# Adding the second results to a stored output with accumulating memory-to-memory transfers

## Chip, cores and metric

The kernel runs on one core of one Trainium2 chip. The metric is the device time of one execution in microseconds (us). Five engines take part: TensorE (PE), VectorE (DVE), ScalarE (ACT), GpSimd (POOL) and SyncE (SP). They run their own instruction streams and wait for one another through semaphores. SP, ACT and POOL also issue DMA transfers.

## What is computed

The input `x` has 16 images of 16 by 16 positions with 128 channels, so 4096 normalised tokens for the expert part: 2 experts of 8 are chosen for each token.

```python
x = x + conv(_ln_c(x))              # attention-like mixing inside each image
t = x.reshape(16, 256, 128)         # x here is called x1 in the kernel
logits = tn @ Wg                    # tn = _ln_t(t)
top_logits, top_idx = top_k(logits, 2);  top_w = softmax(top_logits)
for the two chosen experts e:
    y_e = (silu(tn @ W1[e]) * (tn @ W3[e] + b3[e])) @ W2[e]
out = t + top_w[0] * y_first + top_w[1] * y_second
```

## The kernel before

The first part works through 8 units of 512 tokens (4 tiles of 128): normalisation, mixing, x1, the choice of experts, and a scatter of each token's row, twice, into `sorted_rows` in main memory, ordered by expert. x1 stays in SBUF, in `x1_all`.

The second part runs over 71 slots (`NS`), each a tile of 128 rows of one expert. SP loads the rows of a slot into one of 8 buffers `xs`. TensorE, ScalarE and VectorE compute the expert's result. ScalarE writes the weighted result in two parts (`y_parts`), GpSimd adds the two parts into one of 8 buffers `ys` (L1192) and scatters the 128 rows to `result_rows` in main memory with an indirect DMA (L1195). The semaphore `y_out[b]` counts the scatters of buffer b. `result_rows` holds for each token two rows: the result of its first expert at the token's number, that of its second expert `TOK` = 4096 rows further on.

The experts are worked through in order, and the kernel's structure lets the first half of `result_rows` be complete a few slots before the second: the table `first_half` says how many scatters of each ring buffer must have landed for it.

The last part adds the results to x1 and stores the output. It is the part that the change touches. Its steps are:

- SP waits for the scatters that the first half needs (`half_table`, L472 and on), then issues eight loads of 256 KB (`load_results(u, 0)`, L461), one for each unit, into the tile `both`. That tile lies in the room of the expert weights, `w_all`, which are no longer needed; the profile therefore names it `w_all`. A load on one of four semaphores waits for the load four units earlier.
- VectorE adds each unit's first half to x1 in place (`add_half`, L1143) and counts `half_ready`.
- SP waits for all scatters (L479) and issues eight more loads, of the second half.
- VectorE adds x1 to each of these in place and counts `res_ready`.
- ACT stores each unit (`store`, L852) when its `res_ready` has come, and waits for all stores (`out_done`).

Loads and stores of this part have contiguous pieces of 1 KB: two tokens of 128 floats for each of 128 partitions and two images.

GpSimd has nothing to do after its last scatter. An engine runs its stream in order: GpSimd's scatters of the last slots stand in front of anything that comes behind them.

Of the kernel before, what the change touches and what calls it, by code (L numbers as in the profile page):

```python
# [34 lines left out]
ALU = mybir.AluOpType  # L35
# [3 lines left out]
P = 128  # L39
# [4 lines left out]
def ds(start, size):  # L44
    return slice(start, start + size) if isinstance(start, int) else bass.ds(start, size)
# [33 lines left out]
def build(nc, x, Wq, bq, Wk, bk, Wv, bv, Wr, br, Wg, W1, W2, W3, b3, out):  # L79
    B, H, W, C = x.shape  # L80
    TOK = B * H * W
    NT = TOK // P
    DIM = Wq.shape[1]
    VDIM = Wk.shape[1]
    E, _, F = W1.shape
    TPU = 4
    NU = NT // TPU
    IMG = H * W
    K = 2
    KF = F // P  # L90
    REGION = TOK + P
    NS = (K * TOK + E * (P - 1)) // P
# [3 lines left out]
    RING = 8  # L96
    LAST_RING = 4
# [2 lines left out]
    assert E == NU  # L100

    x_tok = x.rearrange("b h w c -> (b h w) c").rearrange("(b p s) c -> p b (s c)", p=P, s=2)
    out_tok = out.rearrange("b h w c -> (b h w) c").rearrange("(b p s) c -> p b (s c)", p=P, s=2)

    sorted_rows = nc.dram_tensor("sorted_rows", [E * REGION + SPARE * P, ROW], F32)
    result_rows = nc.dram_tensor("result_rows", [K * TOK + (E + SPARE) * P, P], F32)

    with ExitStack() as ctx:
        def sb(name, shape, dt=F32):
            return ctx.enter_context(nc.sbuf_tensor(name, shape, dt))  # L110

        def sem(name):
            return ctx.enter_context(nc.semaphore(name))
# [38 lines left out]
        x1_all = x_all  # L152
# [68 lines left out]

        w_flat = w_all[:].rearrange("p e j f -> p (e j f)")
        UC = TPU * C
        both = w_flat[:, 0:NU * K * UC]
        ys = [w_flat[:, NU * K * UC + i * P:NU * K * UC + (i + 1) * P] for i in range(RING)]
        assert NU * K * UC + RING * P <= E * 3 * F
        y_parts = [sb(f"y_parts{i}", [P, 2, C]) for i in range(2)]


# [84 lines left out]
        y_sum = sem("y_sum")  # L314
        y_out = [sem(f"y_out{i}") for i in range(RING)]

        y_in = [[sem(f"y_in{i}_{k}") for k in range(K)] for i in range(LAST_RING)]
        half_ready = sem("half_ready")
        res_ready = sem("res_ready")
        out_done = sem("out_done")  # L320

        POOL_CONSTS = 8
# [4 lines left out]
        def at_least(eng, semaphore, value):  # L327

            if not (isinstance(value, int) and value <= 0):
                eng.wait_ge(semaphore, value)  # L330
# [59 lines left out]
        @block.sync  # L390
        def _(sp):
            def load_x(u):

                at_least(sp, x_in[u.par], u.half * 16)
                sp.dma_start(x_all[:, ds(u.n * TPU, TPU), :].rearrange("p (b s) c -> p b (s c)", s=2),
                             x_tok[:, ds(u.n * 2, 2), :]).then_inc(x_in[u.par], 16)

            load_x(Step(0, 0))
            for dst, src in ((wkv[:, 0:VDIM], Wk), (wkv[:, VDIM:P], Wv),
                             (bkv[0:VDIM, :], bk.unsqueeze(1)), (bkv[VDIM:P, :], bv.unsqueeze(1))):  # L400
                sp.dma_start(dst, src).then_inc(kv_in, 16)
            for u in range(1, 4):
                load_x(Step(0, u))
            sp.dma_start(w_all[:, :, 0, :], W1.rearrange("e c f -> c e f")).then_inc(expert_in, 16)
            sp.dma_start(w_all[:, :, 1, :], W3.rearrange("e c f -> c e f")).then_inc(expert_in, 16)
            for k in range(KF):
                sp.dma_start(w_all[:, :, 2, k * C:(k + 1) * C],  # L407
                             W2[:, k * P:(k + 1) * P, :].rearrange("e p d -> p e d")).then_inc(expert_in, 16)
            with sp.Fori(2, NU // 2) as q:
                load_x(Step(q, 0))  # L410
                load_x(Step(q, 1))
            sp.dma_start(b3_all[:].rearrange("p e f -> p (e f)"),
                         b3.rearrange("e f -> (e f)").partition_broadcast(P)).then_inc(b3_in, 16)

            sp.wait_ge(pool_consts, POOL_CONSTS)
            for i in range(SPARE):
                first = E * REGION + i * P
                sp.dma_start(sorted_rows[first:first + P, :], pad_rows[:, E + i, :]).then_inc(pads_in, 16)


            def free_rows(u):
                sp.wait_ge(scattered[u.par], u.half * (16 * SCATTERS) + 16 * SCATTERS)
                sp.sem_inc(rows_free, 1)

            sp.sem_inc(rows_free, 2)
            with sp.Fori(0, NU // 2 - 1) as q:
                free_rows(Step(q, 0))
                free_rows(Step(q, 1))

            sp.wait_ge(count_ready, 1)  # L430
            for e in range(E):
                n_rows = sp.value_load(count_i[0:1, e:e + 1], min_val=0, max_val=TOK)
                sp.dma_start(sorted_rows[ds(n_rows + e * REGION, P), :], pad_rows[:, e, :]).then_inc(pads_in, 16)
            sp.wait_ge(table_ready, 1)

            def load_rows(q, b):
                s = q * RING + b

                at_least(sp, y_out[b], q * 16)
                first = sp.value_load(slot_row[0:1, ds(s, 1)], min_val=0, max_val=E * REGION + (SPARE - 1) * P)  # L440
                if isinstance(s, int) and s == 0:

                    sp.wait_ge(pads_in, 16 * (E + SPARE))
                    for i in range(2):
                        sp.wait_ge(scattered[i], 16 * SCATTERS * (NU // 2))
                sp.dma_start(xs[b][:], sorted_rows[ds(first, P), :]).then_inc(xs_in[b], 16)

            for b in range(RING):
                load_rows(0, b)
            with sp.Fori(1, NS // RING) as q:  # L450
                for b in range(RING):
                    load_rows(q, b)
            for b in range(NS % RING):
                load_rows(NS // RING, b)


            def load_results(u, k):

                at_least(sp, y_in[u.ring][k], u.round * 16)
                src = result_rows[ds(u.n * TPU * P + k * TOK, TPU * P), :]  # L460
                sp.dma_start(both[:, ds((u.n * K + k) * UC, UC)].rearrange("p (b m) -> p b m", b=2),  # L461
                             src.rearrange("(b p s) c -> p b (s c)", p=P, s=2)).then_inc(y_in[u.ring][k], 16)

            def load_half(k):
                for o in range(LAST_RING):
                    load_results(Slot(0, o, LAST_RING, NU), k)
                with sp.Fori(1, NU // LAST_RING) as q:
                    for o in range(LAST_RING):
                        load_results(Slot(q, o, LAST_RING, NU), k)


            sp.wait_ge(half_table, 1)  # L472
            for b in range(RING):
                count = sp.value_load(first_half[0:1, b:b + 1], min_val=16, max_val=16 * ((NS + RING - 1) // RING))
                wait_in_front(sp, waited_sp, (y_out[b], count))
            load_half(0)

            for b in range(RING):
                sp.wait_ge(y_out[b], 16 * ((NS - b + RING - 1) // RING))  # L479
            load_half(1)  # L480


        @block.tensor
# [203 lines left out]
        def _(act):  # L687
# [159 lines left out]
            run_slots(act, step, copy_rows_t)  # L847


            def store(u):  # L850
                act.wait_ge(res_ready, u.n + 1)
                act.dma_start(out_tok[:, ds(u.n * 2, 2), :],  # L852
                              both[:, ds((u.n * K + 1) * UC, UC)].rearrange("p (b m) -> p b m", b=2)
                              ).then_inc(out_done, 16)

            with act.Fori(0, NU // 2) as q:
                store(Step(q, 0))
                store(Step(q, 1))
            act.wait_ge(out_done, 16 * NU)


        @block.vector
        def _(dve):
# [270 lines left out]

            run_slots(dve, step, split_rows)

            def add_half(u, k, done):
                x1 = x1_all[:, ds(u.n * TPU, TPU), :].rearrange("p t c -> p (t c)")
                y = both[:, ds((u.n * K + k) * UC, UC)]
                dve.wait_ge(y_in[u.ring][k], u.round * 16 + 16)  # L1140
                if k == 1:
                    dve.wait_ge(half_ready, NU)
                nc.vector.tensor_tensor(y if k == 1 else x1, x1, y, ALU.add).then_inc(done, 1)  # L1143

            for k, done in ((0, half_ready), (1, res_ready)):
                with dve.Fori(0, NU // LAST_RING) as q:
                    for o in range(LAST_RING):
                        add_half(Slot(q, o, LAST_RING, NU), k, done)


        @block.gpsimd
        def _(pool):
# [52 lines left out]
            for n in range(NS // RING * RING, NS):  # L1205
                scatter_results(Slot(0, n, RING, NS))


INPUTS = ("x", "L0_conv_Wq", "L0_conv_bq", "L0_conv_Wk", "L0_conv_bk", "L0_conv_Wv", "L0_conv_bv", "L0_conv_Wr",
          "L0_conv_br", "L0_ffn_Wg", "L0_ffn_W1", "L0_ffn_W2", "L0_ffn_W3", "L0_ffn_b3")  # L1210
# [17 lines left out]
```

## Time and profile before

| | us |
|---|---|
| median of 3 runs | 347.84 |
| lowest, highest | 346.51, 349.89 |
| the profiled execution, its own time | 349.18 |
| its span, first to last instruction | 347.4 |
| last scatter of results issued at | 328.73 |
| last store of the output issued at | 344.8 |

The span is what the trace shows; the execution's own time has a little around it. TensorE is busy for 268.4 us of the span (77%), VectorE 243.7 (70%), ScalarE 183.7 (53%) and GpSimd 176.4 (51%). Times in rows are counted from the span's start. The busy time of a DMA-issuing instruction on SP or ACT says only how long the issue took; when the data landed is told by "DMA to landing".

### The profile page before, as it was taken

The page shows a single profiled execution, that of the slowest core. Times are in us where ns is not written, and L with a number is a line of the kernel's source. Part 1 is how long each engine was busy: PE and PEld are TensorE (multiplying, and loading weights), DVE is VectorE, ACT ScalarE, POOL GpSimd, SP SyncE. Part 2 cuts the span into 40 slices and gives each one's busy share as a digit, 9 for nine tenths or more (in the row PEclk, how much of TensorE's full clock was granted, in tenths as well). Part 3 has the DMA queues.
Part 4 walks back from the last instruction along what each step waited for, and adds up shares of the span by engine and source line. Part 5 has one row for each costly group of instructions (what it writes and reads, how often), then busy time and mean ns, then how long its engine had stood idle before and what let it go on. Part 6 is the DMA issues. An engine that isn't in the chain of part 4 may idle for free.

```text
span 347.4 us, 7832 instructions
## 1 busy us (share of the span) xinstructions
PE 268.4 (77%) x1723; PEld 218.3 (63%) x1724; DVE 243.7 (70%) x811; ACT 183.7 (53%) x464; POOL 176.4 (51%) x221
## 2 busy tenths in 40 slices
PE   1988888868877851869898999999898979989200
PEld 0444555635544531359798999989898969888100
DVE  3357988788897457228687787888787858867633
ACT  3446654645753431026576676767676757766100
POOL 4000055744767757603666666666666556666600
PEclk9999989889999886769999999999999999999755
DMA  3997201101111112320212212211212212123668
GB/s 114 322 311 246 53 27 37 54 31 38 39 40 47 54 33 69 93 55 15 60 49 64 61 52 55 61 54 52 61 53 53 61 46 61 47 61 91 214 214 277
DMA packets 31811, 29.75 MB, mean 86 GB/s; under 512 B 4992, under 2 KB 29504, under 8 KB 31664
## 3 DMA queue, kind: packets, MB, share of 16 engines
q1 hardware_dynamic: 24704, 18.38, 18.7%
q0 software_dynamic: 4320, 8.92, 7.8%
q10 hardware_dynamic: 2768, 2.23, 1.9%
q8 instruction: 7, 0.11, 0.2%
q14 instruction: 12, 0.10, 0.1%
HBM read 17.51 MB, written 12.01 MB: 85 GB/s over the span
## 4 chain that ended last, share of the span: by engine, by line
POOL 22%; PE 21%; issue 19%; DMA 14%; DVE 12%; SPq 6%; ACT 3%; POOLq 1%; DVEq 1%; ACTq 0%
POOL result_rows L1195 11%; POOL w_all L1192 7%; POOL sorted_rows L1175 4%; DMA result_rows<-w_all,xs 4%; DMA xs<-sorted_rows 3%; DMA w_all<-result_rows 3%; PE bank L579 3%; SPq L407 3%; DMA x_all<-x_dram 3%; PE bank L645 2%; PE bank L663 2%; ACT row_buf L742 2%; PE bank L646 2%; PE bank L647 2%; PE bank L539 2%
## 5 line engine op out<-in xcount | busy, mean ns | idle before, releaser
L1175 POOL DMA_INDIRECT sorted_rows<-row_buf,position x64 | 65.1, 1018 | 76.1 <-DVE seen L1020 41.5
L1195 POOL DMA_INDIRECT result_rows<-w_all,xs x71 | 72.2, 1017 | 59.3 <-POOL w_all L1192 57.1
L579 PE MATMUL bank<-all_ones 128*128 128x512 bf16 x205 | 63.7, 422 | 13.3 <-DMA bkv<-L_conv_bv_dram 7.7
L645 PE MATMUL bank<-w_up,xs_hi 128*128 x142 | 55.1, 388 | 7.4 <-issue 7.4
L1098 DVE TENSOR_TENSOR gate<-bank,b_all 128x384 f32<-128x384 f32 x71 | 39.6, 558 | 29.9 <-PE bank L647 29.1
L663 PE MATMUL bank<-w_down,act_hi 128*128 x213 | 58.7, 344 | 0.8 <-ACT y_parts L833 0.8
L647 PE MATMUL bank<-w_up,xs_hi 128*128 x142 | 48.9, 344 | 0.0
L646 PE MATMUL bank<-w_up,xs_lo 128*128 x142 | 48.9, 344 | 0.0
L828 ACT ACTIVATE act_hi<-bank 128x384 fp32r<-128x384 f32 x71 | 34.8, 491 | 26.5 <-PE bank L653 26.1
L665 PE MATMUL bank<-w_down,act_lo 128*128 x213 | 47.6, 223 | 0.0
L1106 DVE TENSOR_TENSOR act_rows<-silu_h,gate 128x384 f32<-128x384 f32 x71 | 44.2, 622 | 3.1
L1192 POOL TENSOR_TENSOR w_all<-y_parts 128x128 f32<-128x128 f32 x71 | 35.4, 498 | 17.3 <-ACT y_parts L833 15.2
L823 ACT ACTIVATE silu_h<-bank 128x384 f32<-128x384 f32 x71 | 34.9, 492 | 15.5 <-PE bank L647 14.9
L579 PEld LDWEIGHTS bank<-all_ones 128*128 128x128 bf16 x205 | 19.7, 109 | 34.0 <-issue 19.1
L663 PEld LDWEIGHTS bank<-w_down,act_hi 128*128 128x128 f32 x213 | 40.1, 188 | 1.3 <-issue 1.1
L665 PEld LDWEIGHTS bank<-w_down,act_lo 128*128 128x128 f32 x213 | 40.8, 192 | 0.0
L833 ACT ACTIVATE y_parts<-bank,xs 128x256 f32<-128x256 f32 x71 | 33.6, 474 | 12.4 <-PE bank L665 10.2
L1118 DVE TENSOR_TENSOR act_lo<-bank,act_hi 128x384 fp32r<-128x384 f32 x71 | 38.9, 548 | 0.7 <-ACT act_hi L828 0.7
L653 PE MATMUL bank<-ident,act_rows 128*128 128x128 f32 x213 | 35.2, 274 | 0.3 <-DVE act_rows L1106 0.3
L645 PEld LDWEIGHTS bank<-w_up,xs_hi 128*128 128x128 f32 x142 | 28.4, 200 | 9.2 <-issue 9.1
L1112 DVE TENSOR_TENSOR xs_lo<-bank,xs_hi 128x128 fp32r<-128x128 f32 x71 | 20.3, 285 | 15.1 <-ACT xs_hi L818 13.2
L742 ACT ACTIVATE row_buf<-x_all,shift,rstd 128x256 f32<-128x256 f32 (+1 forms) x32 | 17.3, 591 | 23.4 <-DVE shift L921 19.5
(137 smaller groups left out, 427.6 us busy)
## 6 DMA issues: line engine op xcount, KB each, us to landing
xs<-sorted_rows SPq DMA_DIRECT2D x71, 65.0 KB
w_all<-result_rows SPq DMA_DIRECT2D x16, 256.0 KB, 4.4
w_all<-L_ffn_W_dram SPq DMA_DIRECT2D x2, 1536.0 KB, 8.8
x_all<-x_dram SPq DMA_DIRECT2D x8, 256.0 KB, 4.0
out_dram<-w_all ACTq DMA_DIRECT2D x8, 256.0 KB, 4.3
w_all<-L_ffn_W_dram SPq DMA_DIRECT2D x3, 512.0 KB, 11.3
b_all<-L_ffn_b_dram SPq DMA_DIRECT2D x1, 1536.0 KB, 8.1
result_rows<-w_all,xs POOLq DMA_INDIRECT x71, 2.3
```

Source lines behind the costliest of these rows:

```text
L579: nc.tensor.matmul(bank[free_bank][:].rearrange("p (a b) -> p a b", a=4), all_ones[:], all_ones[:].unsqueeze(1).broadcast_to([P, 4, P]), s ...
L645: nc.tensor.matmul(o, xs_hi[s.par][:], w[0], start=True, stop=False)
L646: nc.tensor.matmul(o, xs_lo[s.par][:], w[0], start=False, stop=False)
L647: nc.tensor.matmul(o, xs_hi[s.par][:], w[1], start=False, stop=True).then_inc((h_ps, g_ps)[j], 1)
L663: nc.tensor.matmul(bank[7][:, 0:2 * C], act_hi[s.par][:, k * P:(k + 1) * P], w, start=(k == 0), stop=False)
L665: last = nc.tensor.matmul(bank[7][:, 0:C], act_lo[s.par][:, k * P:(k + 1) * P], w[:, 0:C], start=False, stop=(k == KF - 1))
L1098: nc.vector.tensor_tensor(gate[s.par][:], bank[3 + s.par][:, 0:F], b3_all[:, ds(e, 1), :].rearrange("p a f -> p (a f)"), ALU.add).then_inc ...
L1106: nc.vector.tensor_tensor(act_rows[s.par][:], silu_h[s.par][:], gate[s.par][:], ALU.mult).then_inc(act_ready, 1)
L1118: nc.vector.tensor_tensor(act_lo[s.par][:], bank[5 + s.par][:, 0:F], act_hi[s.par][:].bitcast(F32), ALU.subtract).then_inc(act_lo_ready, 1)
L1175: nc.gpsimd.indirect_dma_start(out=sorted_rows.ap(), out_offset=bass.IndirectOffsetOnAxis(ap=position[u.par][:, c:c + 1], axis=0), in_=row ...
L1192: nc.gpsimd.tensor_tensor(ys[s.ring][:], y_parts[s.par][:, 0, :], y_parts[s.par][:, 1, :], ALU.add).then_inc(y_sum, 1)
L1195: nc.gpsimd.indirect_dma_start(out=result_rows.ap(), out_offset=bass.IndirectOffsetOnAxis(ap=xs[s.ring][:].bitcast(I32)[:, DEST:DEST + 1], ...
```

## The change

The second halves are no longer loaded. When VectorE has added the first half of a unit to x1, ACT stores that sum to the output. When all scatters have landed, GpSimd issues for each unit one transfer from `result_rows` straight to the output, in main memory, with `accum_op=ALU.add`: the transfer adds its source to what stands in the output. For unit u it waits for `half_out[u]`, the landing of that unit's store. Each of these transfers covers 256 KB in 128 pieces of 2 KB, contiguous on both sides. GpSimd, and no longer ACT, waits for the end. The loops of ACT and GpSimd over the units are written out.

```diff
-        both = w_flat[:, 0:NU * K * UC]
-        ys = [w_flat[:, NU * K * UC + i * P:NU * K * UC + (i + 1) * P] for i in range(RING)]
+        first_halves = w_flat[:, 0:NU * UC]
+        ys = [w_flat[:, NU * UC + i * P:NU * UC + (i + 1) * P] for i in range(RING)]
...
-            load_half(0)
-
-            for b in range(RING):
-                sp.wait_ge(y_out[b], 16 * ((NS - b + RING - 1) // RING))
-            load_half(1)
+            load_first_half()
...
-            def store(u):
-                act.wait_ge(res_ready, u.n + 1)
-                act.dma_start(out_tok[:, ds(u.n * 2, 2), :],
-                              both[:, ds((u.n * K + 1) * UC, UC)].rearrange("p (b m) -> p b m", b=2)
-                              ).then_inc(out_done, 16)
-
-            with act.Fori(0, NU // 2) as q:
-                store(Step(q, 0))
-                store(Step(q, 1))
-            act.wait_ge(out_done, 16 * NU)
+            for u in range(NU):
+                act.wait_ge(half_ready, u + 1)
+                act.dma_start(out_tok[:, u * 2:u * 2 + 2, :],
+                              x1_all[:, u * TPU:(u + 1) * TPU, :].rearrange("p (b s) c -> p b (s c)", s=2)
+                              ).then_inc(half_out[u], 16)
...
-            for k, done in ((0, half_ready), (1, res_ready)):
-                with dve.Fori(0, NU // LAST_RING) as q:
-                    for o in range(LAST_RING):
-                        add_half(Slot(q, o, LAST_RING, NU), k, done)
+            with dve.Fori(0, NU // LAST_RING) as q:
+                for o in range(LAST_RING):
+                    add_first_half(Slot(q, o, LAST_RING, NU))
...
+            for b in range(RING):
+                pool.wait_ge(y_out[b], 16 * ((NS - b + RING - 1) // RING))
+            for u in range(NU):
+                pool.wait_ge(half_out[u], 16)
+                rows = slice(u * TPU * P, (u + 1) * TPU * P)
+                pool.dma_start(out_rows[rows, :].rearrange("(p s) c -> p (s c)", p=P),
+                               result_rows[TOK + u * TPU * P:TOK + (u + 1) * TPU * P, :]
+                               .rearrange("(p s) c -> p (s c)", p=P), accum_op=ALU.add,
+                               max_dma_last_dim=2048).then_inc(out_done, 16)
+            pool.wait_ge(out_done, 16 * NU)
```

## Rows read from the trace of the kernel before

**Rows 1.** The page: busy tenths in 40 slices of the span

```profile
PE   1988888868877851869898999999898979989200
...
ACT  3446654645753431026576676767676757766100
POOL 4000055744767757603666666666666556666600
...
DMA  3997201101111112320212212211212212123668
```

**Rows 2.** Chain of waits, 327 to 348: start us, us, what

```profile
328.73 2.53 DMA result_rows<-w_all,xs
...
331.40 0.38 SPq L461
...
332.85 4.76 DMA w_all<-result_rows
...
337.63 5.94 DMA w_all<-result_rows
...
343.84 0.69 DVE w_all L1143
```

**Rows 3.** Windows of the end: stretch, length, busy by engine, PEclk, DMA share, GB/s

```profile
324.00:326.00 2.00, 0.03 (x1) 0.00 (x0) 1.59 (x3) 0.47 (x1) 1.38 (x2) 0.76 0.82 252
326.00:328.00 2.00, 0.00 (x0) 0.00 (x0) 1.43 (x3) 0.00 (x0) 1.66 (x2) 0.50 0.69 245
328.00:330.00 2.00, 0.00 (x0) 0.00 (x0) 1.12 (x2) 0.00 (x0) 1.25 (x1) 0.50 0.09 31
...
329.00:330.00 1.00, 0.00 (x0) 0.00 (x0) 0.12 (x1) 0.00 (x0) 0.98 (x1) 0.50 0.00 0
...
330.00:331.30 1.30, 0.00 (x0) 0.00 (x0) 0.00 (x0) 0.00 (x0) 0.00 (x0) 0.50 0.15 50
...
337.60:343.60 6.00, 0.00 (x0) 0.00 (x0) 3.04 (x5) 0.00 (x0) 0.00 (x0) 0.50 1.03 351
```

**Rows 4.** DMA queues in 332.6 to 347.4: packets, MB, share of 16 engines

```profile
DMA packets 4338, 4.18 MB, mean 282 GB/s; under 512 B 256, under 2 KB 4338, under 8 KB 4338
...
q1 hardware_dynamic: 2162, 2.08, 44.4%
q10 hardware_dynamic: 2176, 2.10, 40.2%
```

**Rows 5.** Timeline from 318, and the stores (L852): durations ns, starts, landing

```profile
322.50 1.39 DVE L1143 TENSOR_TENSOR x_all<-x_all,w_all  x2
...
324.07 0.47 ACT L833 ACTIVATE y_parts<-bank,xs 128x256 f32<-128x256 f32 x1 [1.19 <-PE bank L665]
324.40 2.98 DVE L1143 TENSOR_TENSOR x_all<-x_all,w_all  x4 [0.52 <-DMA w_all<-result_rows]
327.83 1.29 DVE L1143 TENSOR_TENSOR x_all<-x_all,w_all  x2 [0.45 <-DMA w_all<-result_rows]
...
L852 ACTq DMA_DIRECT2D out_dram<-w_all x8: 389/391/426, 335.5 to 344.8; - x8
...
DMA to landing us min/median/max: 2.2/4.3/4.9
```

**Rows 6.** Loads (L461); scatters (L1195) from 315 on; the scatter in 318.5 to 319

```profile
L461 SPq DMA_DIRECT2D w_all<-result_rows x16: 372/392/552, 318.4 to 337.6; - x16
...
L1195 POOL DMA_INDIRECT result_rows<-w_all,xs x7: 982/1163/1253, 314.2 to 328.7; - x7
...
DMA to landing us min/median/max: 2.2/3.4/4.5
...
DMA to landing us min/median/max: 4.5/4.5/4.5
```

More of the change, by code:

```diff
@@ L102, in build @@
     x_tok = x.rearrange("b h w c -> (b h w) c").rearrange("(b p s) c -> p b (s c)", p=P, s=2)
+    out_rows = out.rearrange("b h w c -> (b h w) c")
     out_tok = out.rearrange("b h w c -> (b h w) c").rearrange("(b p s) c -> p b (s c)", p=P, s=2)
@@ L223, in build @@
         UC = TPU * C
-        both = w_flat[:, 0:NU * K * UC]
-        ys = [w_flat[:, NU * K * UC + i * P:NU * K * UC + (i + 1) * P] for i in range(RING)]
-        assert NU * K * UC + RING * P <= E * 3 * F
+        first_halves = w_flat[:, 0:NU * UC]
+        ys = [w_flat[:, NU * UC + i * P:NU * UC + (i + 1) * P] for i in range(RING)]
+        assert NU * UC + RING * P <= E * 3 * F
         y_parts = [sb(f"y_parts{i}", [P, 2, C]) for i in range(2)]
@@ L315, in build @@
         y_out = [sem(f"y_out{i}") for i in range(RING)]
-        y_in = [[sem(f"y_in{i}_{k}") for k in range(K)] for i in range(LAST_RING)]
+        y_in = [sem(f"y_in{i}") for i in range(LAST_RING)]
         half_ready = sem("half_ready")
-        res_ready = sem("res_ready")
+        half_out = [sem(f"half_out{i}") for i in range(NU)]
         out_done = sem("out_done")
@@ L454, in _, with load_results, load_first_half @@
                 load_rows(NS // RING, b)
[L457 to L464, printed above, removed]
+            def load_results(u):
+                at_least(sp, y_in[u.ring], u.round * 16)
+                src = result_rows[ds(u.n * TPU * P, TPU * P), :]
+                sp.dma_start(first_halves[:, ds(u.n * UC, UC)].rearrange("p (b m) -> p b m", b=2),
+                             src.rearrange("(b p s) c -> p b (s c)", p=P, s=2)).then_inc(y_in[u.ring], 16)
+            def load_first_half():
                 for o in range(LAST_RING):
-                    load_results(Slot(0, o, LAST_RING, NU), k)
+                    load_results(Slot(0, o, LAST_RING, NU))
                 with sp.Fori(1, NU // LAST_RING) as q:
                     for o in range(LAST_RING):
-                        load_results(Slot(q, o, LAST_RING, NU), k)
+                        load_results(Slot(q, o, LAST_RING, NU))
             sp.wait_ge(half_table, 1)
@@ L1135, in _, with add_first_half @@
             run_slots(dve, step, split_rows)
-            def add_half(u, k, done):
+            def add_first_half(u):
                 x1 = x1_all[:, ds(u.n * TPU, TPU), :].rearrange("p t c -> p (t c)")
[L1139 to L1143, printed above, removed]
-            for k, done in ((0, half_ready), (1, res_ready)):
-                with dve.Fori(0, NU // LAST_RING) as q:
-                    for o in range(LAST_RING):
-                        add_half(Slot(q, o, LAST_RING, NU), k, done)
+                dve.wait_ge(y_in[u.ring], u.round * 16 + 16)
+                nc.vector.tensor_tensor(x1, x1, first_halves[:, ds(u.n * UC, UC)], ALU.add).then_inc(half_ready, 1)
+            with dve.Fori(0, NU // LAST_RING) as q:
+                for o in range(LAST_RING):
+                    add_first_half(Slot(q, o, LAST_RING, NU))
         @block.gpsimd
```

## The prediction

> **What bounds the kernel now.** I read the page first for the shape of the run. In forty slices [rows 1] the DMA engines are lightly used for most of the span and fill up only at its start and in the last four slices, in the last two of which TensorE, ScalarE and GpSimd do nothing. So the end is a stage of its own, and the change touches only it. The chain of waits over the last 20 us [rows 2] says what orders it. GpSimd adds the two parts of a tile (L1192) and scatters its rows (L1195); the last scatter is issued at 328.73 and its data are confirmed 2.53 us later, at 331.26. Only then may SP start reading the second half of the results. It issues eight loads, the chain waits on them (4.76 and 5.94 us), VectorE makes one last addition (0.69 us), and the last store runs out to 347.4. From the landing of the last scatter to the end that is 16.1 us, 4.6% of the span. This is all that the change can shorten.
>
> The windows [rows 3] show what fills these 16.1 us: from 332.6 to the end the DMA engines move 4.18 MB, eight loads of 256 KB and eight stores of as much. By queue [rows 4], SP's loads take 44.4% of 16 engines over these 14.8 us, 6.6 us of full use, and ACT's stores 40.2%, 5.9 us. The transfers alone are 12.5 us; the other 3.6 us are SP's issue and the first latency (331.3 to 332.6), some idle time and the last landing. VectorE's eight additions (L1143) lie beside transfers, but for the last one. In 337.6 to 343.6 the engines are full at 351 GB/s [rows 3]. So the end is bound by bytes, with a latency at each side, and a change in it is to be priced in passes of 2.1 MB over the DMA engines, each about 6 us.
>
> **The change, part by part.** Times are on the clock of the profiled execution (span 347.4); its own time is 349.18, so 1.8 us lie around the span, and the median of the runs is 347.84. I add the difference that I get to the median.
>
> *What goes.* The eight second loads (6.6 us of the engines), the second additions (8 by 0.69 us, of which only the last is on the path) and the eight stores after them (5.9 us). SP's wait for all scatters (L479) goes too. SP has nothing behind it. The smaller buffer `first_halves` moves the scatter buffers `ys` to other columns, which costs nothing.
>
> *What moves: the stores, now of x1 plus the first halves.* They run from ACT after each first addition. ACT's last piece of work ends at 324.07+0.47 = 324.5 [rows 5], two additions are done by then, so the first store goes at about 324.7. The additions go on until 329.12 [rows 5], and the last store goes just behind. VectorE and ACT issue costs (0.39 us a store [rows 5]) lie under the additions. The bytes don't lie under nothing, though: the engines are at a share of 0.82 in 324 to 326 and 0.69 in 326 to 328 with the first loads and scatters, and only 0.09 and 0.15 afterwards [rows 3]. If the store data begin at 326, there is 1.4 us of load and scatter work in 326 to 328, 0.4 us in 328 to 331.3, and 5.9 us of stores: the engines are full until about 326+7.7 = 333.7. No store bounds the end by itself; GpSimd needs `half_out[0]` first, and that was stored long ago.
>
> What it costs is the last scatter, which now lands among stores. Issued at 328.73 it took 2.53 us with idle engines [rows 2]. Of the scatters among the first loads one took 4.5 us, and the median of the last seven is 3.4 [rows 6]. So its landing is 0.9 to 2.0 us later: I take 1.5, at 332.8. If the stores keep out of its way it is 0. Everything queued behind it on GpSimd, all eight accumulating transfers, waits for it. Here the trace agrees with the Trainium skill (DMA: Bandwidth & Descriptors, "Issuing engines are not separate DMA queues"), which says that transfers from all queues run on the same 16 engines and interleave.
>
> *What is added: eight accumulating transfers from GpSimd, memory to memory.* Each moves 256 KB, 128 pieces of 2 KB. The kernel before has none of this kind, so there are two prices to bound.
>
> The first is GpSimd's time for one. From below, SP's and ACT's issue of a 256 KB transfer, 0.39 us [rows 5, 6]; from above, GpSimd's own row that makes 128 addresses, 0.98 us at the least and 1.25 us beside VectorE [rows 2, 6]. VectorE is silent then. I take 1.0 plus 0.15 for the waits and register work between. Eight are 9.2 us.
>
> The second is the time on the DMA engines. An addition must read the source, read the output rows, and write them: two reads and one write for 2.1 MB each. From below it costs one pass, 5.9 to 6.6 us (the second read hidden). From above it costs three, since a load or a store of the kernel before touches main memory once and this touches it three times: 18.8 us. Between these I take two passes, because each engine must read twice what it writes: 12.5 us. That is more than GpSimd's 9.2, so GpSimd runs ahead and its issue is hidden but for the first.
>
> By the Trainium skill (Collectives: The Full Stack, "The bandwidth ceiling: the fold count and why AG ≠ RS ≠ AR") an addition in a transfer halves the rate since it needs two source reads, and the addition itself is free; that is the two passes. No row here shows it.
>
> *The sum.* The last scatter lands at 332.8. The first accumulating transfer's data begin 1.6 us after its issue, as the last scatter's do (issued 328.73, no bytes until 330 [rows 2, 3]): 334.4, when the stores are just gone. Two passes, 12.5 us: 346.9. Idle time in between: before, it was 14.8−12.5 = 2.3 us with VectorE in the loop; here the queue is kept full, I take a quarter, 0.6: 347.5. From the last data to the end of the span, 0.7 us (the last store was issued at 344.8 and took at least 2.2 us to land [rows 5], and the span ends at 347.4): 348.2. Before it is 347.4, so +0.8, and on the median 348.6 us. One latency hop and one pass of stores leave the end; half a microsecond to two come back by the late scatter, and the second read of the output rows eats the pass saved. No change that could be told.
>
> **Rivals.** *The addition costs one pass (chance 0.24).* If the second read hides under the write, the data take 6.3 us and GpSimd's issue is the bound: 332.8 + 7 × 1.15 = 340.9 for the last issue, then 2.2 us as the last store took, 0.9 more for GpSimd's slower issue, and 0.4 to the end: 344.4, that is −3.0 and 344.8 us. With an issue of 0.45 us the data bind: 334.4+6.3+0.7 = 341.4, 341.8 us; with 1.25 us and gaps of 0.15 it is 346.5 us. For it: loads and stores together ran at 351 GB/s, so reading and writing do go on at once. Against: nothing shows one engine reading two streams at that rate. Somewhat over half of this case lies beyond 1%.
>
> *Memory traffic binds (chance 0.34), the case on the other side.* Place: the eight accumulating transfers. If every touch of main memory costs what it did before, three passes are 18.8 us: 334.4+18.8+0.7 = 353.9, +6.5, 354.3 us. It makes the kernel slower by over 1% once the data take 16 us or more, under 131 GB/s of results. For it: in the kernel before no transfer goes from memory to memory, so the 351 GB/s were never asked of memory alone; the 128 pieces of a transfer also each wait for a read before the write can go. Against: if the two sides of memory are not shared with the engines' own limit, the third touch is free. The Trainium skill (DMA: Bandwidth & Descriptors, "Latency and other measured facts") has plain copies between memory tensors at 207 to 214 GB/s in each direction at best. At that rate one plain copy of 2.1 MB would be 10 us and three touches instead of two 15 us, which would end about 3 us later than before. No run here shows it.
>
> *Something else (0.06)*: the addition works off one piece after another at well over three passes.
>
> **How the numbers follow.** My forecast (two passes) has 0.36: 348.6 us, on its own 345.5 to 351.5, the low end with the scatter on time, no idle time and data 8% faster, the high one with the scatter 0.5 us later still, 1.2 us more idle time and data 10% slower. One percent of the median, about what a measurement of this kernel can tell from no change, is 3.5 us: 344.4 and 351.3. Faster by over 1%: 0.15 from one pass and 0.05 from the forecast, 0.20. Slower by over 1%: 0.29 from three passes, 0.06 from the last case and 0.03 from the forecast, 0.38. Within: 0.42. The range runs from 343.5 (a one-pass addition with a cheap issue, beyond which I leave some 0.08) to 356 (three passes with the late scatter at its worst, beyond which 0.10).
>
> **What the profile after would show.** ACT's stores from about 324.7 to 329.6, and DMA share near 1 until 333 or so. The last scatter landing 3.4 to 4.5 us after its issue instead of 2.53. Eight GpSimd transfers about 1.15 us apart from 332.9. Then the stretch from the first accumulating data to the last: near 6 to 9 us is one pass, 12 to 13 two, 18 or more three. If GpSimd's issues lie more than 1.6 us apart, it is GpSimd that binds, which I give little room. My forecast is wrong above all if that stretch is not 12.5 us; a scatter that is not late moves it by 1.5 us.

## The result and the profile after

The changed kernel is slower. Its median is 352.93 us (351.24 to 355.08, 4 runs) against 347.55 us (346.51 to 349.89, 4 runs) of the kernel before, a ratio of 1.0193 with a 95% interval of 1.0138 to 1.0248. The ratio is estimated from the fast runs and is not the quotient of the two medians, which is 1.0155. The time lies inside the whole forecast range (343.5 to 356), but above the forecast of 348.6 us, above that forecast's own 345.5 to 351.5, and above the 351.3 us up to which the prediction spoke of no change.

The page of the kernel after shows busy tenths in 40 slices of a span of 349.2 us, as [rows 1] does for the kernel before:

```profile
POOL 4000055745767677216666666666666566666530
DMA  4998101111111113211122122122212121229790
```

The last digit of the DMA row is a 0. For the last slice, 8.7 us, almost nothing is transferred, and no engine computes, yet the span goes on. The chain of waits (start us, us, what) in 322 to 350, to be compared with [rows 2], ends at 334.9 and says nothing of the last 14 us:

```profile
322.77 4.40 DMA result_rows<-w_all,xs
...
327.98 6.89 POOL out_dram L1201 x8
```

The windows of the same trace, columns as in [rows 3]:

```profile
322.80:327.20 4.40, 0.00 (x0) 0.00 (x0) 1.38 (x2) 0.00 (x0) 0.96 (x1) 0.50 1.07 379
327.20:330.00 2.80, 0.00 (x0) 0.00 (x0) 0.00 (x0) 0.00 (x0) 2.02 (x4) 0.50 0.26 35
330.00:341.60 11.60, 0.00 (x0) 0.00 (x0) 0.00 (x0) 0.00 (x0) 4.87 (x6) 0.50 1.00 178
341.60:349.20 7.60, 0.00 (x0) 0.00 (x0) 0.00 (x0) 0.00 (x0) 0.00 (x0) 0.50 0.00 0
```

The accumulating transfers fill the engines from 330 to 341.6 at 178 GB/s of results, and then 7.6 us follow with nothing at all. What these are is told by the sequencers' own instructions on the line of the closing block. Columns: line, engine, instruction, count, duration in ns least/median/most, first and last start. First after, then before, and with the latter GpSimd's last scatter (start us, us):

```profile
L109 POOLq COMPARE_BRANCH  x1: 38/38/38, 341.6 to 341.6; - x1
L109 POOLq DRAIN  x1: 7176/7176/7176, 341.8 to 341.8; - x1
```

```profile
L108 POOLq DRAIN  x1: 8012/8012/8012, 328.5 to 328.5; - x1
...
L108 ACTq COMPARE_BRANCH  x1: 38/38/38, 347.0 to 347.0; - x1
L108 ACTq DRAIN  x1: 8/8/8, 347.2 to 347.2; - x1
...
328.73 1.25 POOL L1195 DMA_INDIRECT result_rows<-w_all,xs  x1 [0.81 <-POOL w_all L1192]
```

Each engine ends its program with an instruction called DRAIN, the closing drain. On ACT it took 8 ns in the kernel before, on GpSimd 7 to 8 us. In the kernel before GpSimd's sequencer took up the drain at 328.5, while the last scatter still stood in front of it; the scatter's row ends at 330.0, and the drain was through at 336.5, 6.5 us later and eleven microseconds before the end. In the changed kernel GpSimd is the engine that waits for the last transfers (`out_done`), so its drain starts after them, at 341.8, and nothing lies beside it.

The stretch from the issue of the last scatter to the end of the span, step by step:

| us | before | after | difference |
|---|---|---|---|
| last scatter, issue to landing | 2.5 | 4.4 | +1.9 |
| landing to the next transfer's issue | 0.1 | 0.8 | +0.7 |
| that issue to the last landing | 15.6 | 13.6 | −2.0 |
| last landing to the end of the span | 0.4 | 7.6 | +7.2 |
| sum | 18.7 | 26.4 | +7.7 |

The accumulating transfers did save 2 us here. The late scatter took them back, and the drain costs 7.2. The stretch is 7.7 us longer, but the spans differ by only 1.8 (349.2 and 347.4). In this execution of the changed kernel the last scatter was issued 6.0 us sooner, at 322.77. Nothing before it was changed, and experiment e8 treats it.

### The profile page after: what moved, and what is told of

It is laid out like the page before. It is cut to its first block, busy times and chain, and to the rows that moved or that the text cites. A ratio compares the mean times of both kernels' runs of the same rounds, so it can differ in the third digit from the quotient of the medians.

```text
span 349.2 us, 7747 instructions
## 1 busy us (share of the span) xinstructions
PE 265.1 (76%) x1723; PEld 215.3 (62%) x1724; DVE 239.1 (68%) x803; ACT 183.7 (53%) x464; POOL 183.9 (53%) x229
## 3 DMA queue, kind: packets, MB, share of 16 engines
q0 software_dynamic: 5472, 11.02, 11.2%
## 4 chain that ended last, share of the span: by engine, by line
POOL 32%; issue 23%; PE 14%; DVE 12%; DMA 9%; ACT 4%; POOLq 1%; SPq 1%; DVEq 1%; ACTq 0%
POOL result_rows L1183 15%; POOL w_all L1180 9%; POOL sorted_rows L1163 5%; PE bank L576 4%; DMA result_rows<-w_all,xs 3%; DMA xs<-sorted_rows 2%; DMA sorted_rows<-row_buf,position 2%; POOL out_dram L1201 2%; ACT row_buf L739 2%; DMA bkv<-L_conv_bv_dram 1%; DVE stats L886 1%; PE bank L526 1%; DVE x_all L950 1%; PE bank L501 1%; DVE stats L875 1%
## 5 line engine op out<-in xcount | busy, mean ns | idle before, releaser
L576 PE MATMUL bank<-all_ones 128*128 128x512 bf16 x205 | 62.8, 417 | 13.0 <-DMA bkv<-L_conv_bv_dram 7.6
L642 PE MATMUL bank<-w_up,xs_hi 128*128 x142 | 54.4, 383 | 7.2 <-issue 7.2
L644 PE MATMUL bank<-w_up,xs_hi 128*128 x142 | 48.5, 341 | 0.0
L1098 DVE TENSOR_TENSOR act_rows<-silu_h,gate 128x384 f32<-128x384 f32 x71 | 45.0, 634 | 3.1
L820 ACT ACTIVATE silu_h<-bank 128x384 f32<-128x384 f32 x71 | 35.0, 493 | 13.8 <-PE bank L644 12.3
L1104 DVE TENSOR_TENSOR xs_lo<-bank,xs_hi 128x128 fp32r<-128x128 f32 x71 | 20.2, 284 | 15.3 <-ACT xs_hi L815 12.5
L739 ACT ACTIVATE row_buf<-x_all,shift,rstd 128x256 f32<-128x256 f32 (+1 forms) x32 | 17.3, 590 | 23.7 <-DVE shift L913 16.1
```

The lines of the kernel that those rows point to most:

```text
L576: nc.tensor.matmul(bank[free_bank][:].rearrange("p (a b) -> p a b", a=4), all_ones[:], all_ones[:].unsqueeze(1).broadcast_to([P, 4, P]), s ...
L642: nc.tensor.matmul(o, xs_hi[s.par][:], w[0], start=True, stop=False)
L644: nc.tensor.matmul(o, xs_hi[s.par][:], w[1], start=False, stop=True).then_inc((h_ps, g_ps)[j], 1)
L1098: nc.vector.tensor_tensor(act_rows[s.par][:], silu_h[s.par][:], gate[s.par][:], ALU.mult).then_inc(act_ready, 1)
```

## Experiments

Each kernel's times stand beside runs of the kernel before on the same chip. The level differs: beside e1 to e4 and e9b the kernel before took about 370 us, beside the others 347 to 348, and the granted clock of the profiled runs is 0.86 to 0.88 there against 0.90 to 0.92. The difference arises before the first result scatter, which is issued at 182.8 to 185.8 in the traces of the 370 us level and at 156.4 to 162.9 in the others; from there to the last one it takes 165 to 168 us at both. What sets the level isn't known. The stretch from the last scatter's issue to the end has hardly any TensorE work in it, and I compare that across the levels ("the end stretch" below: 18.7 us before, 26.4 after). It and the ratio answer one question in two ways. The kernel before was traced once, at the 348 us level; e2 and e9b show how far the same transfers can differ from it. All the numbers first (us, but for the ratio):

| kernel | median, before beside it | ratio (95%) | last scatter issued, span | end stretch |
|---|---|---|---|---|
| e1 | 376.48, 369.86 | 1.0165 (1.0112 to 1.0217) | 353.6, 375.9 | 22.3 |
| e2 | 377.60, 369.86 | 1.0224 (1.0177 to 1.0271) | 353.0, 377.2 | 24.2 |
| e3 | 373.88, 369.86 | 1.0129 (1.0064 to 1.0195) | 350.0, 371.4 | 21.4 |
| e4 | 377.04, 369.86 | 1.0202 (1.0154 to 1.0250) | 350.2, 376.1 | 25.9 |
| e5 | 355.08, 347.81 | 1.0165 (1.0096 to 1.0234) | 328.7, 353.2 | 24.5 |
| e6 | 347.42, 347.81 | 0.9974 (0.9933 to 1.0016) | 326.8, 345.9 | 19.1 |
| e7 | 353.84, 347.81 | one run, none | 325.3, 351.8 | 26.5 |
| e8 | 354.99, 347.81 | 1.0178 (1.0123 to 1.0234) | 326.9, 353.1 | 26.2 |
| e10 | 350.33, 347.45 | 1.0076 (1.0021 to 1.0131) | 328.3, 347.7 | 19.4 |
| e9b | 371.27, 370.78 | 1.0010 (0.9975 to 1.0044) | 353.2, 371.0 | 17.8 |

### e2: the closing drain exposed in the kernel before

```diff
-            act.wait_ge(out_done, 16 * NU)
...
+            pool.wait_ge(out_done, 16 * NU)
```

> The kernel before, with one edit: the wait for the stores of the output stands on GpSimd instead of ACT. No transfer and no computation is changed. Theory (closing drain): GpSimd's drain of 7 to 8 us now begins when the last store has landed, so the kernel is slower by about 7 us, 2.0%: near 355 us. Rival a (drain takes its time only for transfers in flight; none are left by then): under 1 us slower. Rival b: no change.

One wait was moved from one engine to another, and the kernel became 2.2% slower (at least 1.8%). The closing instructions in its trace:

```profile
L108 POOLq COMPARE_BRANCH  x1: 38/38/38, 370.3 to 370.3; - x1
L108 POOLq DRAIN  x1: 6527/6527/6527, 370.5 to 370.5; - x1
```

The last store has landed at 370.3, and the drain still takes 6.5 us though GpSimd has nothing in flight. The end stretch is 24.2 us, 5.5 more than in the kernel before; the medians differ by 7.7. The stretch has two parts. From the last store's landing to the end of the span it is 6.9 us against 0.4. From the last scatter's issue to that landing it is 17.3 us against 18.3, a microsecond less with the same transfers. Both rivals fall, and this edit alone has the size of the whole loss. For the saving of the change it says this: loads and stores take 14.7 us here from the first load's issue to the last landing, and 15.6 in the trace before, so the changed kernel's 13.6 us save 1 to 2 us.

### e1: ACT waits for the accumulating transfers

```diff
                               ).then_inc(half_out[u], 16)
+            act.wait_ge(out_done, 16 * NU)
...
-            pool.wait_ge(out_done, 16 * NU)
```

> The changed kernel, but ACT and not GpSimd waits for the accumulating transfers. Theory (closing drain): in the changed kernel GpSimd's closing drain of 7.2 us stands behind its wait for the transfers, with nothing beside it; here it begins when the last transfer is issued (334.9 in the changed kernel's trace, landing 341.6) and lies beside the data. If the drain runs its course from the last issue, as in the kernel before (it ended 6.5 us after the last scatter was issued), it ends near 342 and the kernel is 6 to 7 us faster than the changed one: about 345 us. Rival a (the drain starts its work only when GpSimd's own transfers have landed): the end stays within 1.5 us of the changed kernel. Rival b (the drain has no part in the slower time, the accumulating transfers alone are dear): no change to the changed kernel, 352 us.

The end stretch fell from 26.4 to 22.3 us: by 4, not by 6 to 7, and not by under 1.5 either. The ratio of 1.0165 overlaps that of the changed kernel, so it doesn't separate the two, and e4, with the changed kernel's end on the same chip, is only 0.6 us slower in its median. The trace shows why my expectation failed. The landing row is that of the accumulating transfers, in us:

```profile
L109 POOLq DRAIN  x1: 14472/14472/14472, 361.2 to 361.2; - x1
L109 ACTq COMPARE_BRANCH  x1: 38/38/38, 372.0 to 372.0; - x1
...
L1202 POOL DMA_DIRECT2D out_dram<-result_rows x8: 973/1940/3051, 358.3 to 362.2; - x8
...
DMA to landing us min/median/max: 4.1/6.9/9.9
```

ACT is through at 372.0. GpSimd's drain began at 361.2 and ends at 375.7, 3.6 us after GpSimd's own last transfer landed (362.2+9.9 = 372.1). So this drain did not end before GpSimd's transfers had landed, and had some 3.6 us left then. With GpSimd's as the last transfer of the kernel, 3.6 us stay exposed though ACT waits.

### e4: does the drain pay for each transfer?

```diff
             scatter_rows(Step(0, NU - 1))
+            pool.drain()
```

> The changed kernel with one more drain on GpSimd, after its scatters of sorted rows (64 of them), where it idles for 14 us. It tells what the closing drain's 7.2 us are for. Theory (the drain works through each transfer that GpSimd issued since the last drain, 143 in the changed kernel, about 50 ns each): the closing drain falls to 79/143 of 7.2 us, 4.0 us, the early one takes about 3 us where it is hidden, and the kernel is 3.2 us faster than the changed one. Rival (a fixed price for each drain): the closing drain stays at 7.2 us, the kernel at its time; slower, if the early drain delays the first result scatter.

```profile
L1175 POOLq DRAIN  x1: 13992/13992/13992, 154.5 to 154.5; - x1
```

```profile
L109 POOLq DRAIN  x1: 6516/6516/6516, 369.3 to 369.3; - x1
```

The closing drain took 6.5 us with 79 transfers since the last one, and the same 6.5 us with 135 in e2; with 143 it took 7.2. The theory wanted 4.0 and a price in proportion to the transfers, and that is refuted. The early one began at 154.5 while scatters were still queued in front of it (the last one started at 162.2 and took 0.96 us) and was through at 168.5, 5.3 us later, well before the first result scatter at 185.0. It cost nothing that can be seen (end stretch 25.9), and it brought nothing. A fixed price isn't shown either: from GpSimd going free to the end of the drain it took 5.3 us with 64 transfers since the last drain, 6.5 with 79 or 135, and 7.2 with 143.

### e3: plain copies, the addition of the second halves left out

```diff
-                               .rearrange("(p s) c -> p (s c)", p=P), accum_op=ALU.add,
+                               .rearrange("(p s) c -> p (s c)", p=P),
```

> The changed kernel with plain copies in place of the accumulating ones: the addition of the second halves is left out, the output is the second half alone. Theory (an addition costs two passes over the DMA engines, a copy one): the share of the engines that GpSimd's eight transfers take falls from 12.1 us to about 6 us, GpSimd's issue (0.98 us at least, eight of them) becomes the bound of this stretch, and the end is 3 to 4 us sooner. Rival (memory traffic or the pieces of 2 KB set the pace, not the second read): under 2 us sooner, the rate stays near 200 GB/s.

GpSimd's queue in e3, from the first issue to the last landing (354.1 to 364), and below it the same of the changed kernel (327.9 to 341.7). Columns: packets, MB, share of 16 engines:

```profile
q0 software_dynamic: 640, 2.10, 60.0%
```

```profile
q0 software_dynamic: 1152, 2.10, 87.4%
```

A copy takes 60.0% of 9.9 us, 5.9 us of full use; an addition 87.4% of 13.8 us, 12.1 us. That is a factor of 2.03. From memory to memory a copy costs no more than a load or a store of the same bytes did before (5.9 to 6.6 us, from [rows 4]), and the addition costs one more pass. One rival remains in these two rows: the copies also went in fewer packets (640 against 1152). e7 meets it. First issue to last landing fell from 13.6 to 9.7 us, 3.9 as the theory said. The issue row of the copies shows that GpSimd was not the bound even then:

```profile
L1201 POOL DMA_DIRECT2D out_dram<-result_rows x8: 526/526/592, 354.2 to 357.9; - x8
```

They start 0.53 us apart. The expectation had named GpSimd's issue as the bound at 0.98 us each; that part is wrong.

### e7: pieces of 8 KB

```diff
-                pool.dma_start(out_rows[rows, :].rearrange("(p s) c -> p (s c)", p=P),
+                pool.dma_start(out_rows[rows, :].rearrange("(p s) c -> p (s c)", p=32),
                                result_rows[TOK + u * TPU * P:TOK + (u + 1) * TPU * P, :]
-                               .rearrange("(p s) c -> p (s c)", p=P), accum_op=ALU.add,
-                               max_dma_last_dim=2048).then_inc(out_done, 16)
+                               .rearrange("(p s) c -> p (s c)", p=32), accum_op=ALU.add,
+                               max_dma_last_dim=8192).then_inc(out_done, 16)
```

> The changed kernel with the accumulating transfers in 32 pieces of 8 KB instead of 128 of 2 KB. Theory (the price is the two reads): the engines' use stays near 12 us, the landing of the last transfer 13 to 14 us after the first issue. Rival (the price is per piece): a fourth of the pieces cuts it below 9 us. A fourth of the pieces also cuts what GpSimd's part of each transfer takes. If the closing drain depends on the number of pieces in GpSimd's queue it falls below 6 us; if it is a fixed price it stays at 6.5 to 7.2.

With a fourth of the pieces the transfers take 78.8% of 14.2 us, 11.2 us of full use instead of 12.1, and the last one lands 14.1 us after the first issue (344.2 against 330.1). The closing drain is 7.2 us. The queue's packets fell from 1152 to 384, fewer than the 640 of e3's copies, and yet the engines were used for 1.9 times as long as by the copies. So neither pieces nor packets explain the second pass; they move the price by 7%, and the time not at all. GpSimd's part of a single transfer hardly changed either (0.93 us at the least against 0.98).

### e5: without the early stores (the output lacks x1 plus the first halves)

```diff
-            for u in range(NU):
-                act.wait_ge(half_ready, u + 1)
-                act.dma_start(out_tok[:, u * 2:u * 2 + 2, :],
-                              x1_all[:, u * TPU:(u + 1) * TPU, :].rearrange("p (b s) c -> p b (s c)", s=2)
-                              ).then_inc(half_out[u], 16)
+            act.wait_ge(half_ready, NU)
...
-                pool.wait_ge(half_out[u], 16)
```

> The changed kernel with ACT's stores of x1 plus the first halves left out (the output lacks that part) and GpSimd's waits for them gone. Theory (the last scatter lands late because stores fill the DMA engines): it lands 2.5 us after its issue, as in the kernel before, and not 4.4 as in the changed kernel; the eight accumulating transfers are unchanged at 12.1 us of the engines, and from the last scatter's issue to the end of the span it takes 24 to 24.5 us instead of 26.4. Rival (the lateness comes from the first loads, or from chance): the landing stays at 3.4 to 4.5 us.

The chain of waits of e5:

```profile
328.72 2.50 DMA result_rows<-w_all,xs
```

Without the stores the last scatter lands 2.50 us after its issue, as in the kernel before (2.53, [rows 2]); with all of them it took 4.4, 3.9 (e1), 3.4 (e3), 4.4 (e4), 4.0 (e7) and 3.9 (e8). The end stretch is 24.5 us. So the stores beside it delay the last scatter by 0.9 to 1.9 us. This is the price of storing early.

### e8: the changed kernel again

No edit.

> The changed kernel unchanged, beside the kernel before on the same chip. In the first trace of it the last scatter was issued 6.0 us sooner than in the trace before, though nothing before it was changed. Theory (these 6.0 us are chance, from the granted clock of the earlier stages, and the change costs what the stretch after the last scatter's issue shows): the ratio is that of 26.4 against 18.7 us, 7.7 us or 2.1 to 2.2%, and the stretch is 26.4 within 0.5 us. Rival (the earlier stages are really faster with the changed kernel, by 6 us): the ratio is 1.005.

The end stretch is 26.2 us and the ratio 1.0178, which is 6.2 us, with 4.3 to 8.1 as its interval; the 7.7 us of the end stretch lie inside. In this trace the last scatter is issued at 326.9, in the first trace of the same code at 322.8, in that of the kernel before at 328.7. The place of the last scatter moves by 4 us between two executions of one code, and the ratio does not have the 1.005 that a really faster start would give. Most of the 6.0 us lie far ahead of the change, as the scatters of results show (first and last start; first trace, then e8; the kernel before begins at 161.3):

```profile
L1183 POOL DMA_INDIRECT result_rows<-w_all,xs x71: 982/985/1367, 156.4 to 322.8; - x71
...
L1183 POOL DMA_INDIRECT result_rows<-w_all,xs x71: 982/982/1363, 161.4 to 326.9; - x71
```

4.9 us of the 6.0 were there before the first result was scattered. They come from no edit and did not return in e8: chance. The expectation put them down to the granted clock, but its mean is 0.918 in the first trace and 0.919 in that of the kernel before. What set them stays open.

### e6 and e10: two or four of eight units by GpSimd, ACT waits for the end

```diff
+        BY_POOL = 2
...
+            for u in range(BY_POOL, NU):
+                sp.dma_start(second_halves[:, u * UC:(u + 1) * UC].rearrange("p (b m) -> p b m", b=2),
...
+            act.wait_ge(res_out, 16 * (NU - BY_POOL))
+            act.wait_ge(out_done, 16 * BY_POOL)
...
-            for u in range(NU):
+            for u in range(BY_POOL):
                 pool.wait_ge(half_out[u], 16)
```

In e10 `BY_POOL` is 4. ACT's early stores run over the first `BY_POOL` units as well, and the other units' second halves go through SP, VectorE and ACT as in the kernel before.

> A mix meant to keep the changed kernel's gain without the exposed drain: units 0 and 1 go the changed kernel's way (stored early, accumulating transfer from GpSimd, 2 of 8), units 2 to 7 the way of the kernel before (second half loaded, added by VectorE, stored by ACT); ACT waits for the end. Theory (closing drain, and two passes either way): GpSimd is free 13 us before the end, its drain is hidden, the late scatter costs under 1 us more than in the kernel before, and the last scatter's issue to the end takes 17.5 to 18.5 us against 18.7 before: within 0.5% of the kernel before, and 2% faster than the changed one. Rival (GpSimd's transfers share the engines and land late, and 3.6 us of drain follow them): 20 us or more.

> The mix with four units instead of two by GpSimd's accumulating transfers. Theory (the closing drain cannot end sooner than 3.6 us after GpSimd's last transfer has landed): GpSimd's transfers share the engines with loads and stores and land within 2 us of the last store, so 2 to 3.5 us of the drain are exposed, and the last scatter's issue to the end takes 20.5 to 22 us against 19.1 with two units. Rival (the drain is hidden whenever ACT is the one that waits): 19 us.

The closing instructions, e6 and then e10:

```profile
L109 POOLq DRAIN  x1: 12673/12673/12673, 330.4 to 330.4; - x1
L109 ACTq COMPARE_BRANCH  x1: 38/38/38, 345.5 to 345.5; - x1
```

```profile
L109 POOLq DRAIN  x1: 14801/14801/14801, 332.7 to 332.7; - x1
L109 ACTq COMPARE_BRANCH  x1: 38/38/38, 346.4 to 346.4; - x1
```

In e6 GpSimd's last transfer lands at 339.7, the drain ends 3.4 us later, at 343.1, and ACT ends the kernel at 345.5: all hidden. Against the changed kernel on the same chip (e8) it is 2.0% faster (0.9974 against 1.0178), and against the kernel before it is no different. Its end stretch, 19.1 us, missed the 17.5 to 18.5 that I expected. In e10 the last transfer lands at 344.0, the drain ends at 347.5, again 3.5 us later, and ACT was done at 346.4. 1.1 us are exposed, where I expected 2 to 3.5, and the end stretch of 19.4 us is below my range. The ratio rose by 1.0% over e6, 3.5 us across two chips, but the end stretch by only 0.3; the rest of that rise isn't explained by the traces. So the drain's place came out as forecast in both traces, and the sizes did not. The last scatter was not late in either (2.41 and 2.39 us) with two or four early stores.

### e9b: a version that might beat both

```diff
-            load_half(1)
+            for u in range(NU):
+                sp.dma_start(both[:, (u * K + 1) * UC:(u * K + 2) * UC].rearrange("p (b m) -> p b m", b=2),
+                             result_rows[TOK + u * TPU * P:TOK + (u + 1) * TPU * P, :]
+                             .rearrange("(b p s) c -> p b (s c)", p=P, s=2)).then_inc(y_in2[u], 16)
```

> The kernel before, with the eight second loads written out and a semaphore for each, so that loads 5 to 8 no longer wait for the landing of loads 1 to 4 (SP waited there for 6.2 us in all). Theory (the end is bound by bytes, 12.5 us of the engines, and only 2.3 us of idle time lie between): the engines stay full, and the last scatter's issue to the end falls from 18.7 to between 17.3 and 18.2 us: 0.1 to 0.4% faster, which may be lost in the measurement. Rival (loads all queued first push the stores behind, and the last store comes no sooner): 18.7 us or more.

VectorE's second additions (not in this excerpt) wait for `y_in2[u]` one by one.

The end stretch is 17.8 us, inside the range, 0.9 below the kernel before. But the gain can't be put down to the edit: its last store lands 17.3 us after the last scatter's issue, and so it does in e2, at the same level, with the loads of the kernel before. The ratio, 1.0010 (0.9975 to 1.0044), shows no difference. 0.9 us of 370 is 0.24%, less than the interval can tell, so whether it is faster stays open. No version tried here beats the kernel before by more than can be measured.

## Why the prediction was right or wrong

The range was met, and that was luck. The forecast put no change first, with its own range up to 351.5 us; the measured 352.93 lies beyond it. It lies in the whole range only because a rival that didn't come true, memory traffic, had stretched that to 356. The parts of the sum were right but for its last step.

**What bounds the end: right.** The end is bound by passes over the DMA engines. I put 12.5 us on two passes, and 12.1 us were measured; a copy took 5.9 (e3). By the Trainium skill (Collectives: The Full Stack, "The bandwidth ceiling: the fold count and why AG ≠ RS ≠ AR") an addition in a collective transfer costs a second source read and not the adding itself. The measured factor agrees: 2.03, and 1.9 with pieces of 8 KB.

**The late scatter: right.** I took 1.5 us in a range of 0.9 to 2.0. It was 1.9 in the profile and 0.9 to 1.9 in the experiments with the same stores, and it goes away with the stores (e5).

**GpSimd's issue: right in its effect, wrong in its size.** I took 1.15 us for each and called it hidden. It is 0.54 us from one to the next ((331.8−328.0)/7); the single rows of 1 to 3 us overlap. That number would have mattered only in the one-pass rival.

**The landing of the last accumulating transfer: right.** From the last scatter's landing the sum has 14.7 us to the end of the data. Measured from there to the last landing are 14.4 us (327.2 to 341.6). Two errors inside nearly cancel. The engines filled up at 330.0, 2.8 us after the scatter's landing where I had 1.6, and then needed 11.6 us where I had 13.1 with idle time; the 0.6 us of idle time did not come, the engines' share in 330 to 341.6 is 1.00.

**The last step of the sum: wrong.** "From the last data to the end of the span, 0.7 us" was taken from the kernel before, where ACT waits for the last transfer. The step carried the tail of one engine over to another. I had noted that GpSimd and no longer ACT waits for the end, and priced it at nothing. From the last landing to the end it was 7.6 us instead of 0.4. That is the whole miss: 348.2 of the sum and 7 us more is 355, and in the first trace the last scatter, 6.0 us early by chance, brought the span down to 349.2. The trace of before had the row that told of it: GpSimd's drain of 8012 ns, started at 328.5. The sum was made from instructions that count as busy, and the drain isn't one of them.

**The rivals.** One pass falls by e3. Memory traffic as a bound falls as well: a memory-to-memory copy ran at the price of a load, and three touches cost two passes. Its time of 354.3 us is near the measured 352.93, but for another reason. Most of my chance of 0.38 for slower by over 1%, 0.29 of it, was put on it, so where that chance came true it was for a wrong mechanism. The rule of the Trainium skill that I set beside this rival (DMA: Bandwidth & Descriptors, "Latency and other measured facts"), 207 to 214 GB/s for copies between memory tensors, would have made a copy of 2.1 MB take 10 us; e3's engines were in use for 5.9 us. Its transfers did span 9.7 us from the first issue to the last landing, but with both latencies in it: from the first landing (357.2) to the last (363.8) the other seven copies, 1.84 MB, came in 6.7 us, 275 GB/s, with 381 GB/s as the highest rate in a slice. The measurement decides: that rate is no ceiling for these copies.

**Open.** Why the closing drain is 6.5 us in some kernels (e2, e4) and 7.2 in others (the changed one, e3, e5, e7, e8) wasn't found. Two bounds fit the closing drains that began with transfers under way. In the kernel before and in e9b it ended 6.5 us after GpSimd's last row, just what e2's took with nothing in flight, and 5.2 us after the scatter's landing. In e1, e6 and e10, in which the landing came 7 to 9 us after GpSimd's last row, it ended 3.4 to 3.6 us after the landing. What it does in that time no row shows. e2's medians differ by 7.7 us and its trace by 5.5. The interval of the ratio reaches down to 6.5 us, which is what the end behind the last landing grew by (6.9 against 0.4); why its loads and stores took a microsecond less than in the trace before wasn't found.

## What to carry to other kernels

Before moving the last wait of a kernel to another engine, read what that engine does after its last instruction: its closing drain can be microseconds on GpSimd, and is hidden only if GpSimd has finished well before the end, which in this kernel meant its last instruction 6.5 us and its last landing 3.6 us ahead. Price an accumulating transfer as two passes of its bytes over the DMA engines and a copy as one, as measured here from memory to memory. Moving an addition from VectorE into a transfer then replaces a load and a store by one transfer of the same price, and saves little when VectorE's work was hidden already. Read the end of the span by the sequencers' own instructions, since rows of busy engines and the chain of waits leave them out.

## What the runs showed of the hardware that was not expected

- A closing drain on GpSimd took 6.5 to 7.2 us with nothing in flight (seven traces: the changed kernel, e2, e3, e4, e5, e7, e8), and the accumulating transfers' pieces, 128 or 32 each, made no difference; on ACT it took 8 to 155 ns. It didn't end before GpSimd's own transfers had landed, and where these landed late it took 3.4 to 3.6 us more (e1, e6, e10).
- Memory-to-memory transfers of 256 KB from GpSimd: as a copy 5.9 us of all 16 engines for 2.1 MB, with addition 12.1 us in pieces of 2 KB and 11.2 in pieces of 8 KB (the changed kernel, e3, e7).
- GpSimd issued such transfers every 0.53 to 0.55 us. As copies each has a row of 0.53 to 0.59 us; with the addition the rows are 0.98 to 3.05 us and overlap.
